# Expert weights loaded into dead SBUF ahead of the expert slots, in one fused kernel of two layers

## What is computed

```python
x = _layernorm(x + _L0_attn_ref(x, ...))      # recurrence
x = _layernorm(x + _L0_ffn_ref(x, ...))       # gated feed-forward, 704 wide
x = _layernorm(x + _L1_attn_ref(x, ...))      # cumulative attention, then a gated one of 1024
x = _layernorm(x + _L1_ffn_ref(x, ...))       # experts

def _L1_ffn_ref(x, W_up, W_gate, W_down, gate_inp):    # E, K = 16, 4; C, H = 256, 448
    logits = xf @ gate_inp.T
    topv, topi = jax.lax.top_k(logits, K)
    w = jax.nn.softmax(topv, axis=-1)
    dense_w = zeros((n, E)).at[arange(n)[:, None], topi].set(w)
    u = jnp.einsum('nc,ehc->neh', xf, W_up)
    g = jnp.einsum('nc,ehc->neh', xf, W_gate)
    return jnp.einsum('neh,ech,ne->nc', jax.nn.silu(g) * u, W_down, dense_w)
```

## Time and profile before

| | us |
|---|---|
| median of 3 timed runs | 2088.32 (2087.14 to 2092.66) |
| the profiled execution | 2071.18 |
| its span, first to last instruction | 2069.3 |
| last instruction of the sequences' part (POOL) | 1401 |
| first DMA of the expert slots (SP) | 1406 |
| PE busy | 1800.3 (87%) |
| bytes moved | 225.49 MB, 109 GB/s over the span |

### The profile page before, as it was taken

How to read it: one execution, slowest core, us unless ns; L and a number is a source line. 1 busy time by engine, 2 the same in 40 slices (tenths; PEclk the granted TensorE clock), 3 DMA queues, 4 the chain that set the end, 5 groups by cost and what they waited for, 6 DMA issues and landing times. The chain is left out here.

```text
span 2069.3 us, 35458 instructions
## 1 busy us (share of the span) xinstructions
PE 1800.3 (87%) x9012; PEld 1265.5 (61%) x9013; DVE 1363.8 (66%) x3020; ACT 770.6 (37%) x1527; POOL 828.4 (40%) x824
## 2 busy tenths in 40 slices
PE   3589999999999999999999998764899999999990
PEld 2357667667667676676576675552466666666660
DVE  3778888878788888887888786331344455544545
ACT  3234344344344344443443442211233333333333
POOL 2122243233333333422422432122466666666664
PEclk8799999999999999999999999876899999999995
DMA  8123133132232231331331321007987777777887
GB/s 287 54 92 107 28 116 91 43 106 73 70 106 62 80 106 42 92 111 35 103 106 27 115 77 48 20 16 237 317 138 135 133 135 137 133 135 133 135 126 249
DMA packets 307465, 225.49 MB, mean 109 GB/s; under 512 B 190736, under 2 KB 286288, under 8 KB 307024
## 3 DMA queue, kind: packets, MB, share of 16 engines
q1 hardware_dynamic: 262352, 153.20, 26.6%
q0 software_dynamic: 40704, 67.40, 16.7%
q10 hardware_dynamic: 4352, 4.20, 0.6%
HBM read 119.23 MB, written 67.73 MB: 90 GB/s over the span
## 5 line engine op out<-in xcount | busy, mean ns | idle before, releaser
L1639 PE MATMUL pu<-w_ug,xh 128*128 x1728 | 362.3, 358 | 13.0 <-issue 9.9
L1778 POOL DMA_INDIRECT sums_dram<-yo,meta_in x144 | 228.4, 1586 | 125.3 <-DVE yo L1744 87.0
L1639 PEld LDWEIGHTS pu<-w_ug,xh 128*128 128x128 bf16 x1728 | 170.1, 99 | 160.6 <-issue 35.3
L795 PE MATMUL pb<-x1T,w_sw 128*128 128x256 f32 x1024 | 229.1, 382 | 0.7 <-ACT x1T L913 0.7
L795 PEld LDWEIGHTS pb<-x1T,w_sw 128*128 128x128 f32 x1024 | 194.6, 191 | 43.6 <-ACT x1T L913 10.6
L1654 PE MATMUL py<-w_dn,hh 112*128 x1728 | 215.5, 275 | 1.4 <-DMA hh<-hs 1.4
L1730 DVE TENSOR_TENSOR hid<-pu,gate 128x448 f32<-128x448 f32 x144 | 90.0, 625 | 168.6 <-PE pu L1639 164.8
L1765 POOL DMA_INDIRECT xin<-x_dram,meta_in x144 | 144.4, 1003 | 115.7 <-DMA meta_in<-meta_dram 52.8
L1654 PEld LDWEIGHTS py<-w_dn,hh 112*128 112x128 bf16 x1728 | 170.1, 99 | 22.1 <-issue 1.7
L611 PE MATMUL pa<-w_in,xT 128*128 128x512 f32 (+1 forms) x384 | 155.3, 549 | 14.6 <-DMA xT<-in_xT 13.9
L1700 ACT ACTIVATE hs<-hid 128x448 bf16<-128x448 f32 x144 | 83.0, 576 | 219.5 <-DVE hid L1730 201.5
(11 more groups left out here) (245 smaller groups left out, 3342.3 us busy)
## 6 DMA issues: line engine op xcount, KB each, us to landing
w_stage<-in_w_ug SPq DMA_DIRECT2D x64, 224.0 KB, 3.5
split_ug<-w_parts SPq DMA_DIRECT2D x64, 224.0 KB, 3.2
w_ug<-split_ug SPq DMA_DIRECT2D x16, 896.0 KB, 7.2
xg_dram<-xg SPq DMA_DIRECT2D x16, 512.0 KB, 3.5
rows<-sums_dram SPq DMA_DIRECT2D x32, 256.0 KB, 5.2
w_stage<-in_w_dn SPq DMA_DIRECT2D x32, 224.0 KB, 3.0
split_dn<-w_parts SPq DMA_DIRECT2D x32, 224.0 KB, 2.8
w_dn<-split_dn SPq DMA_DIRECT2D x16, 448.0 KB, 8.2
```

What stands on the lines that cost most here:

```text
L795: last = mm(pb[:, 1 + j % 2, w * T:(w + 1) * T], w_sw[:, c, o:o + P], x1T[:, c, :], start=c == 0, stop=c == DC - 1)
L1639: last = mm(pu[:, 2 * b + w, 0:EH], xh[:, b, xp, c, :], w_ug[:, bass.ds(e, 1), wp, c, w * EH:(w + 1) * EH], start=n == 0, stop=n == 3 * DC ...
L1778: nc.gpsimd.indirect_dma_start(out=sums_dram[m % 2], out_offset=bass.IndirectOffsetOnAxis(ap=meta[:, m, 0:1], axis=0), in_=yo[:, m % XS, : ...
```

## The change

SBUF of the first block is laid out again. One tensor `w_all` of 16 experts, each 5632 bf16 elements per partition (3584 of `w_ug`, 2048 of `w_dn`), lies at the address where the first block's tensors begin. The tensors that only the A pieces use are allocated first, over experts 0 to 7; then come those that B uses (and the constant matrices), over experts 8 to 10; then those that C and D still need in round 17, with the buffers of the weight pieces. Two assertions hold the borders.

SP gets a new piece `CE` (`load_early`) at the end of its round. In round 16 it waits until all weight pieces are stored and `x1` of sequence 15 is written, and loads experts 0 to 7. In round 17, behind `store_x3` of sequence 15, it loads experts 8 to 10. In the second block `w_all` takes the place of `w_ug` and `w_dn`, and SP loads experts 11 to 15 in one go, between the first four row lists and the first step; the loads in the steps are gone. `load_weights` is a function of the module now, with the same wait of expert e for expert e - 4, and `weights_in` lives through all blocks. Nothing changes on PE, ACT, DVE and POOL.

```diff
+WU, WD = 2 * DC * 2 * EH, 2 * EJ * D
+WB = 2 * (WU + WD)
+EARLY_A, EARLY_B = 8, 11
...
-    "SP": ("C7 A0 N0 A2 WL.0 WL.1 WL.2 WL.3 WL.4 WL.5"),
+    "SP": ("C7 A0 N0 A2 WL.0 WL.1 WL.2 WL.3 WL.4 WL.5 CE"),
...
+        weights_in = [Signal(whole.enter_context(nc.semaphore(f"weights_in{n}")), 32) for n in range(WS)]
+        w_start = nc.sbuf_base
+        w_all = nc.alloc_sbuf_tensor_at("w_all", [P, NE, WU + WD], BF16, offset=w_start)
...
+        assert nc.sbuf_base >= w_start + EARLY_A * WB
+
+        const = sb("const", [P, NMAT, P])
+        w_gate = sb("w_gate", [P, DC, FH])
...
+        assert nc.sbuf_base >= w_start + EARLY_B * WB
+
+        w_route = sb("w_route", [P, DC, NE])
+        x_row = sb("x_row", [P, NT, D])
...
+            def load_early(s):
+
+                if isinstance(s, int) and s >= nseq - 2:
+                    if s == nseq - 2:
+                        for n in range(2):
+                            sp.wait_ge(piece_stored[n].sem, piece_stored[n].at(NE - 1))
+                        sp.wait_ge(x1_ready.sem, x1_ready.at(nseq - 1))
+                    for e in range(*((0, EARLY_A) if s == nseq - 2 else (EARLY_A, EARLY_B))):
+                        load_weights(sp, e, w_all, weights_in, split_ug, split_dn)
...
+def load_weights(sp, e, w_all, weights_in, split_ug, split_dn):
+
+    if e >= WS:
+        sp.wait_ge(weights_in[e % WS].sem, weights_in[e % WS].at(e // WS - 1))
+    sp.dma_start(w_all[:, e, 0:WU], split_ug[e].rearrange("p h c n -> p (h c n)")).then_inc(weights_in[e % WS].sem, 16)
+    sp.dma_start(w_all[0:EC, e, WU:WU + WD], split_dn[e].rearrange("p h j d -> p (h j d)")
+                 ).then_inc(weights_in[e % WS].sem, 16)
...
-            for e in range(3):
-                load_weights(e)
+            for e in range(EARLY_B, NE):
+                load_weights(sp, e, w_all, weights_in, split_ug, split_dn)
...
                 parts(r, m, 0, run=turn_h)
-                if isinstance(r, int) and 3 <= UN * r + m + 4 < NE:
-                    load_weights(UN * r + m + 4)
```

More of the change, by code:

```diff
@@ L247, in build @@
         table = whole.enter_context(nc.sbuf_tensor("table", [1, 2, ntile], I32))
-        layers_block(nc, ins, nseq, cap, ntile, ident, waited, small, base, table, meta_dram, x3_dram, sums_dram, split_ug, split_dn, xg_dram)
-        experts_block(nc, ntok, cap, ntile, ident, waited, small, base, table, meta_dram, x3_dram, sums_dram, split_ug, split_dn)
+        weights_in = [Signal(whole.enter_context(nc.semaphore(f"weights_in{n}")), 32) for n in range(WS)]
+        w_start = nc.sbuf_base
+        w_all = nc.alloc_sbuf_tensor_at("w_all", [P, NE, WU + WD], BF16, offset=w_start)
+        layers_block(nc, ins, nseq, cap, ntile, ident, waited, small, base, table, meta_dram, x3_dram, sums_dram, split_ug, split_dn, xg_dram,
+                     w_all, weights_in, w_start)
+        experts_block(nc, ntok, cap, ntile, ident, waited, small, base, table, meta_dram, x3_dram, sums_dram, split_ug, split_dn,
+                      w_all, weights_in)
         combine_block(nc, nseq, waited, sums_dram, out)
@@ L274, in empty_slots, with layers_block @@
     return m.reshape(P, -1, 4)
-def layers_block(nc, ins, nseq, cap, ntile, ident, waited, small, base, table, meta_dram, x3_dram, sums_dram, split_ug, split_dn, xg_dram):
+def layers_block(nc, ins, nseq, cap, ntile, ident, waited, small, base, table, meta_dram, x3_dram, sums_dram, split_ug, split_dn, xg_dram,
+                 w_all, weights_in, w_start):
     with ExitStack() as ctx:
@@ L346, in layers_block @@
         yss = sb("yss", [P, NT])
-        r1 = sb("r1", [P, NT, D])
-        st1 = sb("st1", [P, NT, 6])
-        mv1 = sb("mv1", [P, NT, 2])
+        assert nc.sbuf_base >= w_start + EARLY_A * WB
+        const = sb("const", [P, NMAT, P])
+        w_gate = sb("w_gate", [P, DC, FH])
+        w_up = sb("w_up", [P, DC, FH])
+        w_down = sb("w_down", [P, FJ, D])
+        s_gu = sb("s_gu", [P, 2, FJ])
+        s_down = sb("s_down", [P, D])
+        w_qkv = sb("w_qkv", [P, DC, 3 * D])
+        w_sw = sb("w_sw", [P, DC, 2 * SH])
+        w_so = sb("w_so", [P, SJ, D])
         x1 = sb("x1", [P, NT, D])
@@ L367, in layers_block @@
         yc = sb("yc", [P, NT, D])
+        assert nc.sbuf_base >= w_start + EARLY_B * WB
+        w_route = sb("w_route", [P, DC, NE])
+        x_row = sb("x_row", [P, NT, D])
+        power = sb("power", [P, 4])
+        r1 = sb("r1", [P, NT, D])
+        st1 = sb("st1", [P, NT, 6])
+        mv1 = sb("mv1", [P, NT, 2])
+        r2 = sb("r2", [P, NT, D])
+        st2 = sb("st2", [P, NT, 6])
+        mv2 = sb("mv2", [P, NT, 2])
         x3 = sb("x3", [P, NT, D])
@@ L1474, in heads, with experts_block @@
     return ap.rearrange("p t (h d) -> p t h d", d=HD)
-def experts_block(nc, ntok, cap, ntile, ident, waited, small, base, table, meta_dram, x3_dram, sums_dram, split_ug, split_dn):
+def load_weights(sp, e, w_all, weights_in, split_ug, split_dn):
[4 more added lines that the diff above has]
+                 ).then_inc(weights_in[e % WS].sem, 16)
+def experts_block(nc, ntok, cap, ntile, ident, waited, small, base, table, meta_dram, x3_dram, sums_dram, split_ug, split_dn, w_all, weights_in):
     with ExitStack() as ctx:
@@ L1484, in sig @@
             return Signal(ctx.enter_context(nc.semaphore(name)), per)
-        w_ug = sb("w_ug", [P, NE, 2, DC, 2 * EH], BF16)
-        w_dn = sb("w_dn", [EC, NE, 2, EJ, D], BF16)
+        sb("w_room", [P, NE, WU + WD], BF16)
+        w_ug = w_all[:, :, 0:WU].rearrange("p e (h c n) -> p e h c n", h=2, c=DC)
+        w_dn = w_all[0:EC, :, WU:WU + WD].rearrange("p e (h j d) -> p e h j d", h=2, j=EJ)
         meta = sb("meta_in", [P, UN, 4], U32)
@@ L1501, in experts_block @@
         ident = ident[:, :]
-        weights_in = [sig(f"weights_in{n}", 32) for n in range(WS)]
         meta_in = [sig(f"meta_in{n}", 16) for n in range(XS)]
```

24 lines of the change are left out of this document (1 added, 23 removed).

## The result

The changed kernel takes 2072.07 us (median of 5 runs, 2063.59 to 2073.89) against 2089.69 us for the kernel before (5 runs, 2087.14 to 2092.66). The ratio is 0.991, with a 95% interval of 0.9887 to 0.9934, a gain of some 17.6 us (14 to 24 by the interval) where 17.4 were forecast and 2071 us stood for the time.

The account below looks back on a forecast made before the run. The first expert slots were taken as bound by DMA transfers, small ones waiting behind weights, later slots by TensorE. Terms -20.8, +2.9 and +0.5 gave -17.4 us, from 2088.3 to 2070.9 us; range 2064 to 2076 at 70%, 2060 to 2080 at 8 in 10.

Parts of the forecast that it names:

- Removed, -20.8 us: Slots 3 to 19: without weight loads under them they run like slots 20 to 36, saving 20.8 us.
- Moved, +2.9 us: Slot 4's row list waits behind expert 15 in SP's queue, so slot 3's product comes 2.9 us later.
- slots 0 to 2 start earlier: Start of the slots: weights are already there, so slots 0 to 2 start earlier, which buys nothing.
- Added in round 16, 0: Eight expert loads in round 16 run while the DMA engines are nearly idle and cost 0.
- Added in round 17, +0.5: Three expert loads behind the x3 store end about when POOL's last scatter is issued, costing 0.5 us.
- Sum, -17.4: Whole kernel: the forecast terms together save 17.4 us, from 2088.3 to 2070.9 us.
- signs of being wrong: Sequences ending over 3 us later, slot 19's product after 1512 or before 1500, or several-us stalls between slots 4 and 14.
- (a): More is gained: slot 4's row list doesn't wait for expert 15; 2068 us, at the far end 2055; 9%.
- (b): Less is gained: slot 4's gather takes the loaded 8.53 us; 2076.6 us, or 2077 with slower weight loads; 9%.
- (d): Slower: instruction fetches in rounds 16 and 17 wait behind the weight loads, 10.7 us each; 2114 us; 5%.
- (c): No difference: (b) plus the last scatter at its upper bound, 2082.3 us, or 2085 to 2088 with PE waits left; 7%.
- SP's turns can be held, at no cost: Early slots: a full queue may hold SP's turns 6.55 us, but later row lists still go out in time; cost nothing.

Follow-up runs that it names:

- before again: The kernel before, unchanged, profiled and timed a second time; ratio 1.0008 to the kernel before.
- the stream doubled: The changed kernel with experts 0 to 7 loaded twice in round 16, one pass after the other; ratio 0.9915 to the kernel before.
- the eight in front: The changed kernel without the three loads of round 17, so experts 8 to 15 are loaded ahead of the slots; ratio 0.9976 to the kernel before.

## Why the prediction was right, step by step

**Removed, -20.8 us.** Slots 3 to 19 took 62.67, 62.62 and 62.75 us in three profiles against 83.61 and 82.97: -20.6. The size was right because the yardstick was a stretch of the same kernel with the same loop edge in it. The prediction tells it as waits for small transfers alone, and that is only a part. Slots 3 to 19 in before, in before again and in after:

```profile
core 0: us, PE busy (x) PEld busy (x) DVE busy (x) ACT busy (x) POOL busy (x), PEclk, DMA share, GB/s
1441.08:1524.69 83.61, 70.22 (x419) 44.14 (x418) 31.62 (x64) 22.54 (x48) 40.70 (x32) 0.90 1.03 266
...
1452.42:1535.39 82.97, 66.55 (x418) 41.81 (x417) 31.61 (x64) 22.62 (x48) 40.65 (x32) 0.96 1.04 270
...
1459.39:1522.06 62.67, 61.59 (x419) 41.47 (x417) 31.61 (x65) 22.26 (x48) 40.09 (x31) 1.00 0.75 128
```

PE stood 13.4 us in before and 1.1 us in after; the other 8.6 of the 20.9 us are the same matmuls at a mean granted clock of 0.90 instead of 1.00. In the second profile of before it stood 16.4 us and was 5.0 us longer busy, at 0.96. So the price of the old order is idle time and a lower clock together, and the difference of two stretches held both without naming the second. The low clock goes along with the waits (0.72 from 1453 to 1477 us in before, with waits for x of 2.94 and 3.57 us); no run sets the two apart.

**Moved, +2.9 us.** Read against the first profile it was +3.8 (38.86 against 35.04). The steps of it held one by one: expert 15 was issued 11.7 us after the first row list (forecast 11.9), the gather of slot 4 began 30.7 us after it (29.8), took 2.84 us, and the product followed 5.32 us later. PE's wait was 12.73 us, where "some 10" stood. The exactness of the last two steps is luck in part: in the second profile of after the gather began 29.2 us after the first list and the product followed the transposition by 4.21 us, with a granted clock of 0.86 in the 10 us after PE's wait instead of 0.74. Over all profiles slot 3 comes at 37.9 us in after and 33.9 in before, so that the term was +4.0, with a spread of 2 to 3 us on either side. That slots 0 to 2 start earlier was wrong: the product of slot 0 came 15.7 us after the first row list, 15.9 in before, since PE waited 4.26 us for x of slot 1 beside the weights; the prediction had given it no value, so the sum doesn't change.

**Added in round 16, 0.** Shown with the stream doubled. It began 4.7 us behind the x3 store of sequence 14, as 1308.8 against 1304.25 had said.

**Added in round 17, +0.5.** 23.20, 23.82 and 23.36 us against 23.22 and 23.18, and 23.20 without these loads: 0 to 0.6. With five loads instead of three it is 3.7, so the tail was indeed where the prediction put it, right at the last scatter.

**Sum, -17.4.** From the x3 store of sequence 14 to slot 19 the profiles give 203.49 against 220.44, -17.0, and over all profiles of both 202.7 against 219.1, -16.4; the times -17.6. That forecast and time agree to 0.2 us is luck: the interval of the ratio reaches from 14 to 24 us, the terms were off by up to about 1 us in both directions, and what comes after slot 19, where nothing was changed, took 544.6 and 547.6 us in the two profiles of before and 549.5, 545.2 and 545.2 in the three of after. The mechanism doesn't hang on it, as the doubled stream and the eight in front show. Two of the prediction's own signs of being wrong came true as they were written: the sequences ended 14.5 us later, and the product of slot 19 stood at 1522.06, after 1512. They were given as times from the start of the span, which the rounds of the loop had moved by 14.3 us; less these 14.3 us slot 19 stands at 1507.7, inside the stated 1500 to 1512. For the same reason the profiled execution took 2073.43 us and not the 2053.8 of the prediction.

**The rivals.** (a) fell with the 12.73 us, (b) with the gather's 2.84, (d) with the doubled stream (its argument from the products counted 16 under full load; the timeline has 14 before 1500). (c) would have needed both (b) and a dear scatter. "SP's turns can be held, at no cost" was right for the order of after (7.96 us, unnoticed) and would have been wrong with the row lists moved ahead, where the same turns became the longest wait. What the prediction didn't see: the median of before was 17 us above its profile mostly because that execution had quick rounds, not because of the slots. It cost nothing only since the sum was made on differences.

## What to carry to other kernels

Bulk loads in a queue that also carries small transfers cost their whole length to what stands behind them; move them to where nobody waits, and if some must stay, put them in front in one piece rather than between the steps of a pipeline that has just lost its lead. When SBUF is laid out by time of death, look for each tensor's own last reader: splitting one group in two brought nearly as much again as the whole first version (ratios 0.9835 and 0.9826 against 0.9904 to 0.992). Count an engine's busy time as well as its waits: of the 20.9 us between two stretches with the same matmuls 8.6 were longer busy time at a lower granted clock. Compare profiles between landmarks, not by their span.

## What the runs showed of the hardware

A small load on its own queue takes 9.02 us instead of 2.48 while another queue has four experts (5.5 MB) to move. A transposing DMA can hold the engine that issues it: 1.26 us when free, 7.96 us behind five experts in its queue, 10.80 behind eight, and 22.07 for three in a row behind five. What decides the hold was not tried; in the kernel before, with one expert between turns, it was 1.26 to 6.55 us at a DMA share of 1.03 to 1.12. The same 419 matmuls kept PE busy 61.59 us at a granted clock of 1.00, 66.55 at 0.96 and 70.22 at 0.90. A DMA stream into SBUF, 25 us long at share 0.92 or 70 us at 0.94, changed round 16 by less than 0.3 us. Hardware-loop rounds of the same code take 79 to 83 us from one round and one execution to the next.
